# Expert mixture of a graph network on one core: the two-tile unit is handled first, the twelve four-tile units follow

## The reference

```
y = jax.nn.elu(y)                       # end of the third layer; y is the layer's sum over edges
y = layer_norm(y, g_l[i], bt_l[i])
h = y + identity
...
w = jax.nn.softmax(feat @ Wr + br, axis=-1)             # feat is the normalised row
h = jnp.einsum('bfd,edh->bfeh', x, W1) + b1
h = jax.nn.relu(_bn(h, g1, be1, m1, v1))
h = jnp.einsum('bfeh,ehk->bfek', h, W2) + b2
h = jax.nn.relu(_bn(h, g2, be2, m2, v2))
y = jnp.einsum('bfeh,ehd->bfed', h, Wo) + bo
return jnp.einsum('bfed,fe->bfd', y, w)
```

## Time and profile before

| | us |
|---|---|
| runs, median of 3 | 6753.14 (6741.82 to 6756.97) |
| profiled execution | 6749.72 |
| its span | 6747.9 |
| first DVE instruction of the stage | 4044.56 |
| first expert product | 4080.65 |
| first product of the two-tile unit | 4994.08 |
| next stage's first DMA | 5042.45 |

### The profile page before, as it was taken

The page is one execution under the profiler, slowest core; times in us unless marked ns, Lnnn a source line. Parts: engine busy times, 40 slices in busy tenths (PEclk is TensorE's granted clock), DMA queues, the critical chain, the costliest instruction groups (busy, mean ns, idle before and its releaser), DMA issues. The chain is left out here.

```text
span 6747.9 us, 97821 instructions
## 1 busy us (share of the span) xinstructions
PE 5290.4 (78%) x22256; PEld 3728.3 (55%) x22256; DVE 4764.2 (71%) x13068; ACT 3945.6 (58%) x13294; POOL 3528.1 (52%) x3571
## 2 busy tenths in 40 slices
PE   1758888845788888458888878999989787777798
PEld 1634445424455555335555547888874566565446
DVE  5756666685677777847777768888871587777793
ACT  4558888874788888648888874444436322111142
POOL 3377777717777776277777740000000577777501
PEclk8878888876899999669999988999999898888899
DMA  6355555435444444454444435555557534333402
GB/s 185 115 151 137 144 140 143 132 103 156 122 124 124 123 128 108 125 144 122 124 126 124 123 82 189 189 190 195 191 189 268 175 117 125 109 108 101 124 2 78
DMA packets 511899, 919.90 MB, mean 136 GB/s; under 512 B 89659, under 2 KB 345611, under 8 KB 511435
## 3 DMA queue, kind: packets, MB, share of 16 engines
q0 software_dynamic: 166320, 446.82, 24.5%
q1 hardware_dynamic: 345259, 469.88, 21.4%
HBM read 773.29 MB, written 152.30 MB: 137 GB/s over the span
## 5 line engine op out<-in xcount | busy, mean ns | idle before, releaser
L1826 POOL DMA_INDIRECT gm_got<-scratch_feat,keep_src_tab x2490 | 2386.6, 958 | 778.5 <-issue 675.0
L2048 ACT ACTIVATE gm_got<-gm_got 128x64 f32<-128x64 f32 x9804 | 2386.6, 337 | 5.3 <-DVE gm_got L1962 5.3
L2104 PE MATMUL gm_bank<-gm_got,gm_onehot 128*128 128x264 f32 x4980 | 1776.2, 455 | 451.0 <-DVE gat_acc L1986 271.9
L2104 PEld LDWEIGHTS gm_bank<-gm_got,gm_onehot 128*128 128x128 f32 x4980 | 881.8, 209 | 1066.6 <-ACT gm_got L2048 691.8
L1986 DVE TENSOR_TENSOR gat_acc<-gat_acc,gm_bank 128x264 f32 x2490 | 1055.7, 424 | 477.1 <-PE gm_bank L2104 198.6
L1114 POOL DMA_INDIRECT mix1a_got<-scratch_rel_feat,layer_rel_tab x240 | 237.9, 991 | 1361.7 <-issue 1360.2
L1114 POOL DMA_INDIRECT mix1b_got<-scratch_rel_feat,layer_rel_tab x590 | 592.9, 1005 | 192.7 <-issue 188.4
L1993 DVE TENSOR_TENSOR gm_onehot<-gm_iota,keep_dst_tab 128x640 f32<-128x640 f32 x498 | 405.5, 814 | 184.8 <-PE gm_bank L2104 181.8
L1171 PE MATMUL mix1b_m_bank<-mix1b_got,mix1b_onehot 128*128 128x256 f32 x1180 | 382.0, 460 | 154.5 <-DVE logit_acc L1145 133.2
L837 POOL DMA_INDIRECT scratch_first<-gat_scores,keep_first_pos x150 | 216.4, 1443 | 486.6 <-DVE gat_scores L820 445.1
L1171 PEld LDWEIGHTS mix1b_m_bank<-mix1b_got,mix1b_onehot 128*128 128x128 f32 x1180 | 243.9, 224 | 259.9 <-DVE mix1b_onehot L1123 151.5
(11 more groups left out here) (578 smaller groups left out, 9538.3 us busy)
## 6 DMA issues: line engine op xcount, KB each, us to landing
moe_w<-scratch_ffn_cut SPq DMA_DIRECT2D x312, 512.0 KB, 3.3
scratch_rel_feat<-rel_out SPq DMA_DIRECT2D x50, 1024.0 KB, 5.2
gm_got<-scratch_feat,keep_src_tab POOLq DMA_INDIRECT x2490, 2.8
gm_flags<-scratch_flags SPq DMA_DIRECT2D x84, 300.0 KB
scratch_feat<-gf_row SPq DMA_DIRECT2D x50, 260.0 KB, 4.1
gm_x<-scratch_x SPq DMA_DIRECT2D x50, 256.0 KB, 3.3
gf_feat<-scratch_feat SPq DMA_DIRECT2D x50, 256.0 KB, 3.9
gf_old<-scratch_hidden SPq DMA_DIRECT2D x50, 256.0 KB, 5.0
```

What stands on the lines that cost most here:

```text
L1826: nc.gpsimd.indirect_dma_start(out=got[:, place // GROUPS, place % GROUPS * GROUP + j, 0:GAT_ROW], out_offset=None, in_=dram["feat"][layer ...
L2048: last = nc.scalar.activation(rows, rows, ACT.Copy, scale=got[:, b, i, D + h:D + h + 1])
L2104: nc.tensor.matmul(bank[i % BANKS][:, 0:GAT_SUM], onehot[:, i % HOTS, :], got[:, v[1] % B, i, :], start=True, stop=True).then_inc(s_sum, 1)
```

## The change

The unit of two tiles becomes unit 0, and the twelve units of four follow as 1 to 12. `size_of` returns `REST` for unit 0 and `QUAD` for all others; new functions `tile_of` and `tiles_at` give the first tile and the tiles of a unit (0, 2, 6, 10, ...). Everything that stood ahead of the units with `QUAD` tiles now stands there with `REST`. `all_units` writes unit 0 out ahead of the loop; the loop runs units 1 to 10, units 11 and 12 stand behind it.

```diff
         def size_of(u):
-            return QUAD if u < N_U - 1 else REST
+            return QUAD if u else REST
+
+        def tile_of(u):
+            return u * QUAD - (QUAD - REST) if u else 0
+
+        def tiles_at(u):
+            return slice(tile_of(u), tile_of(u) + size_of(u))
...
         def all_units(engine, unit, count=None):
 
+            unit(1, 0, 0, tile_of(1), REST, QUAD)
             with engine.Fori(0, LOOPED // 2) as r:
                 if count:
                     count.enter(r, 2 * STEPS)
-                for s in range(2):
-                    unit(r * 2 + (s + 1), s, r * (2 * E) + s * E, r * (2 * QUAD) + (s + 1) * QUAD)
+                for u in (1, 2):
+                    unit(r * 2 + (u + 1), u % 2, r * (2 * E) + u * E, r * (2 * QUAD) + tile_of(u + 1))
             if count:
                 count.leave(LOOPED // 2)
-            for u in range(LOOPED, N_U):
-                unit(u + 1, u % 2, u * E, (u + 1) * QUAD, size_of(u), size_of(u + 1) if u + 1 < N_U else 0)
+            for u in range(LOOPED + 1, N_U):
+                unit(u + 1, u % 2, u * E, tile_of(u + 1), QUAD, QUAD if u + 1 < N_U else 0)
...
                 def store(u):
                     sp.wait_ge(s_done, u + 1)
-                    sp.dma_start(out_tiles[:, u * QUAD:u * QUAD + size_of(u), :], x[:, u % 2, 0:size_of(u), :]).then_inc(s_sent[u % 2], 16)
+                    sp.dma_start(out_tiles[:, tiles_at(u), :], x[:, u % 2, 0:size_of(u), :]).then_inc(s_sent[u % 2], 16)
...
-                edge_part(None, 0, QUAD)
-                own_part(1, QUAD)
+                edge_part(None, 0, REST)
+                own_part(1, REST)
...
-                turn(1, 0, QUAD)
+                turn(1, 0, REST)
```

More of the change, by code:

```diff
@@ L3129, in load_x @@
                 def load_x(u):
-                    sp.dma_start(x[:, u % 2, 0:size_of(u), :], tiles[:, u * QUAD:u * QUAD + size_of(u), :]).then_inc(s_x[u % 2], 16)
+                    sp.dma_start(x[:, u % 2, 0:size_of(u), :], tiles[:, tiles_at(u), :]).then_inc(s_x[u % 2], 16)
                 def load_feat(u):
-                    sp.dma_start(feat[:, 0:size_of(u), :], feats[:, u * QUAD:u * QUAD + size_of(u), 0:D]).then_inc(s_feat, 16)
+                    sp.dma_start(feat[:, 0:size_of(u), :], feats[:, tiles_at(u), 0:D]).then_inc(s_feat, 16)
                 def load_old(u):
-                    sp.dma_start(old[:, 0:size_of(u), :], hidden[:, u * QUAD:u * QUAD + size_of(u), :]).then_inc(s_old, 16)
+                    sp.dma_start(old[:, 0:size_of(u), :], hidden[:, tiles_at(u), :]).then_inc(s_old, 16)
                 def load_weight(j, e):
@@ L3359, in _ @@
                 dve.sem_inc(s_var, 1)
-                elu_norm(1, QUAD)
-                add_rows(1, 0, 16, QUAD)
-                front_statistics(0, QUAD)
+                elu_norm(1, REST)
+                add_rows(1, 0, 16, REST)
+                front_statistics(0, REST)
                 dve.wait_ge(s_root, 1)
@@ L3368, in _ @@
                 nc.vector.tensor_tensor(shift[:, :, :], shift[:, :, :], par[:, :, 2, :], ALU.add).then_inc(s_scale, 1)
-                front_end(1, 0, QUAD)
+                front_end(1, 0, REST)
                 dve.wait_ge(s_w, 16 * len(loads))
                 dve.sem_inc(s_acc, 2)
-                cut_rows(1, QUAD)
+                cut_rows(1, REST)
                 all_units(dve, unit, c)
@@ L3437, in unit @@
                             elu(n + 1, after)
-                scale_own(1, 0, QUAD)
-                elu(1, QUAD)
+                scale_own(1, 0, REST)
+                elu(1, REST)
                 act.wait_ge(s_var, 1)
                 nc.scalar.activation(shift[:, :, :], par[:, :, 4, :], ACT.Sqrt, bias=bn_eps[:, 0:1]).then_inc(s_root, 1)
-                root(1, QUAD)
-                front_root(1, QUAD)
-                turned(1, QUAD)
+                root(1, REST)
+                front_root(1, REST)
+                turned(1, REST)
                 act.wait_ge(s_scale, 1)
```

## The result

| | before | after |
|---|---|---|
| median of 8 runs, us | 6752.4 (6741.82 to 6766.86) | 6768.56 (6759.59 to 6772.84) |
| profiled execution | 6749.72 | 6764.79 |
| from the stage's first DMA to the next stage's | 997.93 | 1014.00 |

The ratio is 1.0023 [1.0014, 1.0032]: the kernel became slower by some 16 us. The two traces say the same: the stage is 16.1 us longer (997.93 = 5042.45 - 4044.52, the first from the earlier trace rows). Outside it the two executions differ by +2.2 us ahead of the stage and -3.3 behind, in parts that are the same code. In the kernel after, the lines of this stage are numbered seven higher.

The account below looks back on a forecast made before the run. PE was taken to set the time of a full unit (busy 72.73 of 75.30 us). The terms -8.8 + 9.6 + 1.5 = +2.3 us, added to the median of 6753.14, gave 6755.4; forecast 6755.5, range 6743 to 6767.

Parts of the forecast that it names:

- (c): Last unit, now four tiles with nothing following: 71.7 us to its last accumulation; the eleven other four-tile intervals unchanged.
- (e): PE's clock falls to half at waits, 1.5 us each; eight places again, give or take four: 6 us either way.
- (a): Preparation ahead of the first unit has half its tiles: 8.8 us less, bounds 7 and 10.5; its starting point doesn't move.
- (b): Two-tile unit beside the preparation of four tiles: 54.7 us to the next unit's first product, bounds 49 and 58.
- second(5): Product of expert 5 in the two-tile unit, after DVE's 4.4 us of row sums: start forecast at 33.2 us.
- third(7): Last third product of the two-tile unit: start forecast at 51.4 us, then 1.5 for itself and 1.85 for routing.
- (d): Last store of the stage is 512 KB instead of 256: 1.5 us more, between 0 and 2.9.
- (1): Rival: PE's clock stays low through the two-tile unit, sum +13.3 us, total 6766; chance 0.09.
- (2): Rival: the preparation hides in the two-tile unit, which takes 40.4 us; sum -12.0, total 6741; chance 0.05.
- (3): Rival: the stage's start doesn't shorten, as the first product waits for weights; sum +9, total 6762; chance 0.08.
- (4): Rival: the places of clock falls decide, none or sixteen hit, 12 us either way: 6743 or 6767; chance 0.09.
- (5): Rival: the change doesn't do what it says, a semaphore count ordering a buffer late in every unit; chance 0.01.

Follow-up runs that it names:

- b_two: Kernel before with its loop over units 1 to 10 instead of 0 to 9, same order, no instruction added: 6773.28 us, ratio 1.0020.
- a_both: Kernel after with do-nothing instructions on PE and DVE that put both loops back at the places of the kernel before: 6755.22 us, ratio 1.0009.
- a_good: Kernel after with both loops at the places of before, the later do-nothing instructions standing where their engine is idle: 6762.35 us, ratio 1.0001.
- a_pe: Kernel after with PE's loop alone moved back to its place before by do-nothing instructions, DVE's left: 6764.65 us, ratio 1.0019.

## Why the prediction was wrong

The prediction said 6755.5 us, 6743 to 6767, and a chance of 0.87 for no measurable difference. It became 6768.6, slower, past the end of the range.

**The step that failed** is the last sentence of (c), "The eleven intervals of four tiles followed by four are eleven before and after", together with (e). They are eleven, and of the same instructions, but not the same: +15.3 us. I read this part for what the engines compute and wait for, found nothing changed, and didn't ask where the loop's code lies. The change writes a unit out ahead of the loop; "The change" says so, and the prediction gave it no price. What the runs put in its place: the loop's body, moved by the unit ahead of it, is fetched anew at each turn on PE and DVE; of the 15.3 us, 5.4 are PE's waits and 9.9 slower products. Moving the loops back takes away 13.2 of them, moving them in the kernel before adds 13.8, and both with the packets that the trace counts; `b_two` moves PE's loop without an added instruction and gets 10.5 of them. The step could have been taken: the instruction queues are rows of the page of the profile (q14 248 packets, q8 72).

**(e), the clock**: "Nothing in the order tells hit places from others" is refuted in part. In the kernel after all four turns with a wait are followed by the lower level. The lower clock isn't a cause of its own here: with the loops in place and the order as changed, PE's products take 815.8 us (`a_both`), against 814.1 before and 824.0 after. What remains open in it is some us: `a_both` and `a_good` have the same placement and differ by 5.9 us in PE's busy time (815.8 and 809.9). My 6 us for it had the right size, for that part only. For PE's misplaced loop alone the slower products cost twice as much as the waits (11.2 and 5.6).

**The terms of the sum** held. (a): 13.31 us against 13.35 from the first copy to the first product. The point at which the preparation starts did move, by 1.7 us, as the 10.5 of the bound had it (0.75 MB less is queued ahead). (b): 55.72 against 54.7, DVE busy 43.3 of it against 44. The path held too: second(5) starts 33.55 us after the unit's first product (33.2 in the prediction), first(7) at 38.20 (38.6) and third(7) at 50.07 (51.4). What the sum left out is the clock. It is 0.87 over this unit, at the lower level in the unit's first 6 us and again from about 4106 and about 4123 on (the upper bound, 58, had two falls), and third(7) and the routing took 5.65 us instead of 3.35. In `a_good`, with a clock of 0.93, the same unit took 53.27. So it is luck that the total came within 1.0 us: the path was 1.3 us shorter than forecast, the clock cost 2.3.

```profile
4072.32:4128.04 55.72, 48.15 (x320) 45.18 (x320) 43.26 (x94) 26.47 (x57) 0.00 (x0) 0.87 0.72 245
...
4106.00:4108.00 2.00, 2.00 (x10) 2.00 (x11) 1.93 (x6) 0.00 (x0) 0.00 (x0) 0.50 0.95 328
...
4124.00:4126.00 2.00, 2.00 (x12) 2.00 (x11) 0.88 (x2) 0.00 (x0) 0.00 (x0) 0.50 0.06 10
```

(c): 71.64 against 71.7. (d): 0.75 against 1.5, half of what I took; the estimate of 0.7 that the prediction worked out from the Trainium skill (DMA: Bandwidth & Descriptors, "Latency and other measured facts") agrees with this. Sum +0.8 in the first pair of traces, with 2.3 forecast; by the kernels without a loop it is 3.6 without the intervals (156.6 against 153.1 us, means of two), mainly because the stall at expert 3 of the earlier trace rows is smaller there (1.10 us instead of 2.87, and 1.66 in the other trace) when the two-tile unit comes last.

**The rivals.** (1), PE's clock low through the two-tile unit, would have given 6766, near the result, but isn't what happened: 55.7 us and a clock of 0.87. The mechanism it took, a wait and behind it slower products, did show, at the turns of the loop. (2) and (3) are refuted by the 55.7 and the 13.3 us. (4), the clock's places with 6767, had the size and the wrong reason. In (5) I looked for a semaphore that orders late in every unit; what repeated was in every turn, and no semaphore. The Trainium skill (Runtime: NRT & Kernel Launch, "Instruction fetch mechanics"), quoted under theory 1, describes a branch whose target isn't held. Here the traces agree with that sentence, at 1.3 to 1.8 us a turn on PE for most of its waits. The same section of the Trainium skill counts on two blocks held, and by that every jump over a body of more than two blocks would be a fetch. The traces don't bear this out for PE: in the kernel before, a body of 1711 instructions was kept through all four jumps, and whether it is depends on where it begins (kept at 249, but for one jump of `a_good`, and not at 65, 105 and 177).

**What stays open.** Which places are good was seen at few points only. The count of seven and eight blocks, above, fits them and wasn't tested, and it doesn't say why `a_good` lost the body in one turn of four.

**Not every "issue" is a fetch.** In the two-tile unit PE stands 2.59 us for "issue" ahead of second(5), in all nine traces with this order, with a loop or without (2.58 to 2.60). This product begins at 4105.87, 0.10 us behind the end of the DVE cut that it reads (4105.08 + 0.69 = 4105.77), and 0.10 to 0.11 us behind it in the other eight traces with this order too. So it is the wait for DVE's row sums that the prediction has at expert 4, and the name alone doesn't show a fetch; at the turns it is the packets that do.

## What to carry to other kernels

Where an edit adds, removes or moves code ahead of a hardware loop, the loop's place in the instruction memory is part of the edit: look at the instruction queues of the DMA section before and after, and for waits for "issue" at the first instruction of a turn; either alone isn't enough. If the packets rise by the body's size for every turn, shift the loop, take another unit as its first, or write it out, before anything is concluded on the edit itself; here the same reordering came out at 1.0023 with one placement and at 1.0001 with another. A short wait on PE then costs more than its length, since the products behind it run at the lower clock.

## What the runs showed of the hardware that I had not expected

- A loop body of 1711 PE instructions ran four jumps without a fetch at one place in three of four kernels (in the fourth one jump fetched), and was fetched again at every jump at three others: 9 packets of 16.4 KB a turn, and PE stood 0.3 to 1.8 us at the jump; at one place it stood twice, 4.5 us together.
- DVE stood longer at a jump than PE, 3.5 to 4.2 us a turn instead of 0.8 at a change without a jump, for a body of 338 instructions (`a_pe`).
- Thirteen units in a row, with 43 packets on PE's queue, caused no wait at a change of units, and a unit written out took 74.94 us against 75.29 in the loop.
- A do-nothing instruction isn't free: 96 of them on DVE and 112 on PE behind the units delayed the next stage by 6 to 7 us, and 96 ahead of DVE's preparation the first product by 6 us.
- One of the chips took 7900 us for all of these kernels, with some 790 us more ahead of this stage and 390 us more behind it, while the stage had its usual length.
